# Decay exponents of a state-space layer: four products per tile instead of twelve, fed by small copies inside the on-chip memory

## The chip, the cores and the metric

The kernel runs on one core of a Trainium2 chip. The metric is the device time of one execution in microseconds, as the median over several runs. A profile was taken of one execution; its times count from the start of that execution's span. The engines are TensorE (PE, with its weight loads as PEld), VectorE (DVE), ScalarE (ACT), GpSimd (POOL) and SyncE (SP), which only issues transfers here. A "q" behind an engine's name is that engine's own queue of instructions that aren't computation.

## The reference

The input is 8 images of 32 x 32 positions with 128 channels, that is 8 sequences of 1024 tokens. Three layers follow each other.

1. A convolution layer with 1 x 1 kernels whose output attends to itself: q and v are two linear maps of the input, the scores are q times q transposed, and out = softmax(scores) v * gamma + input.
2. A state-space layer ("Mamba 2") over the normalised tokens, in residual form. Eight heads of 32 channels, a state of 32 per channel:

```python
def step(state, inp):
    dA_t, dt_t, B_t, C_t, x_t = inp
    state = state * dA_t[:, :, None, None] + (dt_t[:, :, None] * x_t)[..., None] * B_t[:, None, None, :]
    y = jnp.einsum('bhpn,bn->bhp', state, C_t)
    return (state, y)
```

with dA = exp(dt * -exp(A_log)), after a causal convolution over four tokens and a SiLU, and followed by a gated RMS norm and an output projection.

3. A mixture of 8 experts, the best two per token, with SiLU gating, again in residual form.

## The kernel before

The 8192 tokens are worked as 64 tiles of 128 tokens; 8 tiles (NT) make one sequence, called a batch here. Each engine runs its own program, with semaphores between them, and all of them walk through the same list of steps: step i of batch `base` does the scores of tile i, and, for tiles further back, the later stages. With i counted within the batch, `o = i - 1` is the tile of the attention output, `k = i - 6` the tile of the state-space products, `e = i - 7` the tile of its output, and in odd steps `d = i - 5` is the first of a pair of tiles whose decay sums are prepared. The order of the work within a step is written out by hand, engine by engine, and each engine runs strictly in that order.

The recurrence is worked in blocks of one tile. Within a tile, the contribution of key s to query t of head h carries the factor exp(cum[h, t] - cum[h, s]) for s <= t and 0 otherwise, where cum is the running sum of the decay exponents. The exponents for a whole tile are a matrix of 128 keys (partitions) by 8 heads x 128 queries, which TensorE makes in the PSUM bank pair pY; ScalarE exponentiates it into ED (L706); VectorE multiplies it with the tile's key-query products GT into M (L1365); TensorE uses the eight heads of M as weights against XDT (L433), adds the skip term (L437), and VectorE makes Y2 of it (L1266 or L1268), GpSimd YG.

The sums come in three bfloat16 parts that add up to the full value: C3 (VectorE, L1344 to L1358) is transposed by TensorE (L515), so that the three parts of 2 tiles x 8 heads lie on 48 partitions, and ScalarE copies it out twice, as CT3 (L715) and with the sign turned as NCT3 (L716), which raises the semaphore `ct3_ready`. This happens in an odd step; the two tiles of the pair use it in the next even and the next odd step.

Before the change the exponents are made by 12 matmuls per tile, at L454 to L460. Four matmuls of 256 columns have NCT3 as weights and the constant `pickm` as moving data: rows 0 to 47 pick the head's three parts, so that they add -cum[h, s] for every query, and rows 64 to 127 hold, for each half of the queries, a part of the mask: -1e30 where the key lies behind the query. Eight matmuls of 128 columns, one per head, have the constant `pick` as weights and CT3 as moving data, and add cum[h, t] for every key.

GpSimd builds all constants at the start (L829 to L883) and raises `consts` (identity and triangle), `masks` (awaited by ScalarE before its first step) and `iotas` (awaited by VectorE before its first step). SP's program (L249 to L368) loads the inputs, then, batch by batch, the next batch's xT once the present one's v product is done (`load_xT`) and the two halves of its X as the tiles of the attention output are finished (`x0_loaded`, `x1_loaded`); after the batches it fills the padding of the rows sorted by expert (`fill_up`, L307), fetches those rows for the experts (L322) and later the results for the final sum (L337). In the first part of the expert stage the last steps of the list are interleaved.

Other lines that are spoken of: the scores (L412 to L414) into pX, their maximum by VectorE (NM, L1243), the exponentials PR (ScalarE, L677), their transposes (L399) into pY, copied to PT (L648), the attention output (L483), the next batch's q product (L377) with its two parts QH (ScalarE, L637) and QL (VectorE, L1027), the transposes of YG (L467) copied to YT (ScalarE, L709), the output projection (L506), and the norm of two tiles, XN (ScalarE, L691).

Of the kernel before, what the change touches and what calls it, by code (L numbers as in the profile page):

```python
# [5 lines left out]
def conv_attn_ssm_moe(nc, x, xT, dw1, pw1, b1, dw2, pw2, b2, gamma, w_zdt, w_xbc, conv_w, conv_b,  # L6
# [3 lines left out]
    P = 128  # L10
    TILES = x.shape[0] // P
    NT = 8
# [26 lines left out]
    with ctx:  # L39
# [15 lines left out]
        HP = P // 2  # L55
        pickm = sb("pickm", [P, 16, HP], bf16)
        pick = sb("pick", [P, 16, P], bf16)
# [37 lines left out]
        CT3, NCT3 = sb("CT3", [P, 2, P], bf16), sb("NCT3", [P, 2, 2, P], bf16)  # L95
# [5 lines left out]
        ED, M = sb("ED", [P, H, P]), sb("M", [P, H, P])  # L101
# [61 lines left out]
        heads = lambda a: a[:].rearrange("p h t -> p (h t)")  # L163
        Y01 = [[PR[:], PT[:]], [heads(ED), heads(M)], [TR[:].rearrange("p t c -> p (t c)"), X[:].rearrange("p t c -> p (t c)")],
# [85 lines left out]
        def _(sp):  # L250
# [43 lines left out]
            for base in range(0, TILES - NT, NT):  # L294
                load_xT(base // NT + 1)
                sp.wait_ge(s("t_ready"), base + NT // 2)
                sp.dma_start(X[:, 0:NT // 2, :], xtok[:, base + NT:base + NT + NT // 2, :]).then_inc(s("x0_loaded"), 16)
                sp.wait_ge(s("t_ready"), base + NT)
                sp.dma_start(X[:, NT // 2:, :], xtok[:, base + NT + NT // 2:base + 2 * NT, :]).then_inc(s("x1_loaded"), 16)
# [71 lines left out]
        def _(pe):  # L371
# [13 lines left out]
            def step(base, i):  # L385
# [240 lines left out]
        def _(act):  # L626
# [12 lines left out]
            def step(base, i):  # L639
# [64 lines left out]
                if there(base, k):  # L704
                    upto(act, "d_ps", base, k + 1)
                    A(ED[:].rearrange("p h t -> p (h t)"), pY[:], ACT.Exp).then_inc(s("expD_ready"), 1)  # L706
# [123 lines left out]
        def _(pool):  # L830
# [8 lines left out]
            g.memset(pick[:], 0.0).then_inc(s("filled"), 1)  # L839
            pool.wait_ge(s("filled"), 2)  # L840

            g.affine_select(out=tri[:], in_=tri[:], compare_op=ALU.is_ge, fill=0.0, base=0, pattern=[[1, P]], channel_multiplier=-1)
            for j in range(3):
                g.affine_select(out=pick[:], in_=pick[:], compare_op=ALU.not_equal, fill=1.0, base=-16 * j,
                                pattern=[[-1, 16], [0, P]], channel_multiplier=1).then_inc(s("picked"), 1)
                pool.wait_ge(s("picked"), j + 1)
# [4 lines left out]
            g.memset(NCT3[:], 0.0)  # L851
            g.memset(pickm[:], 0.0).then_inc(s("masking"), 1)
            pool.wait_ge(s("masking"), 1)
            for th in range(2):
                last = g.affine_select(out=NCT3[:, :, th, :], in_=NCT3[:, :, th, :], compare_op=ALU.is_ge, fill=-1e30, base=HP * (th - 1),
                                       pattern=[[0, 2], [-1, P]], channel_multiplier=1)
            last.then_inc(s("masking"), 1)
            for j in range(3):
                g.affine_select(out=pickm[:], in_=pickm[:], compare_op=ALU.not_equal, fill=1.0, base=-16 * j,
                                pattern=[[-1, 16], [0, HP]], channel_multiplier=1).then_inc(s("masking"), 1)  # L860
                pool.wait_ge(s("masking"), j + 3)
            g.affine_select(out=pickm[:], in_=pickm[:], compare_op=ALU.not_equal, fill=1.0, base=-HP,
                            pattern=[[0, 16], [-1, HP]], channel_multiplier=1).then_inc(s("masking"), 1)
            pool.wait_ge(s("masking"), 6)
            g.memset(NCT3[0:HP], 0.0).then_inc(s("masks"), 1)
# [152 lines left out]
        def _(dve):  # L1018
# [198 lines left out]
            def step(base, i):  # L1217
# [143 lines left out]
                if there(base, k):  # L1361
# [3 lines left out]
                    tt(M[:], ED[:], GT[:, None, :].broadcast_to([P, H, P]), ALU.mult).then_inc(s("m_ready"), 1)  # L1365
# [208 lines left out]
```

## Time and profile before

| | |
|---|---|
| median of 3 runs | 1214.97 us (1214.96 to 1219.69) |
| span of the profiled execution | 1181.1 us, the only time that the page gives for it |
| TensorE matmul busy | 1083.7 us, 92% of the span |
| VectorE, ScalarE, GpSimd busy | 72%, 64%, 53% |
| first maximum of scores on VectorE | at 23.98 us |
| chain that ended last, by engine | PE 60%, DVE 11%, POOL 10%, issue 10%, ACT 3% |

The runs' time lies 33.9 us above the span: it holds what comes before the first and after the last instruction too. Busy time of TensorE is the time in which a matmul is in the pipeline, and successive matmuls overlap, so that the rows of the chain of waits (where each piece ends where the next begins) give what a matmul costs in sequence. "idle" in a row is the time in which the engine stood before that instruction, with the instruction that released it.

### The profile page before, as it was taken

The page shows a single profiled execution, that of the slowest core. Times are in us where ns is not written, and L with a number is a line of the kernel's source. Part 1 is how long each engine was busy: PE and PEld are TensorE (multiplying, and loading weights), DVE is VectorE, ACT ScalarE, POOL GpSimd, SP SyncE. Part 2 cuts the span into 40 slices and gives each one's busy share as a digit, 9 for nine tenths or more (in the row PEclk, how much of TensorE's full clock was granted, in tenths as well). Part 3 has the DMA queues.
Part 4 walks back from the last instruction along what each step waited for, and adds up shares of the span by engine and source line. Part 5 has one row for each costly group of instructions (what it writes and reads, how often), then busy time and mean ns, then how long its engine had stood idle before and what let it go on. Part 6 is the DMA issues. An engine that isn't in the chain of part 4 may idle for free.

```text
span 1181.1 us, 29643 instructions
## 1 busy us (share of the span) xinstructions
PE 1083.7 (92%) x8432; PEld 998.3 (85%) x8433; DVE 852.1 (72%) x3071; ACT 754.7 (64%) x1903; POOL 624.9 (53%) x981
## 2 busy tenths in 40 slices
PE   3889999999999999999999999867889999999993
PEld 2779888888988988988888888856789999999883
DVE  3488888988988888888898898776355644444564
ACT  1567777777767777767777777742476666666551
POOL 8122444467557566556646655743744665444442
PEclk9999999999999999999999999976799999999997
DMA  7200000001000100100100000010122222223666
GB/s 221 61 1 28 10 2 28 6 24 39 11 25 11 38 19 18 39 20 10 46 6 24 22 13 15 10 28 10 49 60 62 80 78 74 73 64 92 173 181 183
DMA packets 76439, 57.73 MB, mean 49 GB/s; under 512 B 10725, under 2 KB 70669, under 8 KB 76301
## 3 DMA queue, kind: packets, MB, share of 16 engines
q1 hardware_dynamic: 58285, 33.75, 10.5%
q0 software_dynamic: 8704, 17.97, 4.5%
q10 hardware_dynamic: 9312, 4.33, 1.3%
q8 instruction: 66, 1.08, 0.4%
q14 instruction: 72, 0.59, 0.2%
HBM read 32.27 MB, written 24.81 MB: 48 GB/s over the span
## 4 chain that ended last, share of the span: by engine, by line
PE 60%; DVE 11%; POOL 10%; issue 10%; ACT 3%; DMA 2%; SPq 2%; DVEq 1%; POOLq 0%; ACTq 0%
PE pc L433 7%; PE pY L588 7%; PE pX L583 6%; PE pa L483 5%; PE pb L600 3%; PE pd L600 3%; PE pY L399 3%; DVE CV L1232 2%; PE pc L437 2%; POOL rows_by_expert L991 2%; PE pX L412 2%; PE pa L444 2%; PE pX L414 2%; PE pX L413 2%; DMA GX<-rows_by_expert 2%
## 5 line engine op out<-in xcount | busy, mean ns | idle before, releaser
L1003 POOL DMA_INDIRECT results_by_choice<-YE,DIX x144 | 143.2, 995 | 147.6 <-ACT YE L786 132.5
L991 POOL DMA_INDIRECT rows_by_expert<-XA,SL x128 | 147.6, 1153 | 35.2 <-issue 35.2
L1481 DVE TENSOR_TENSOR V<-XT,pY 128x384 f32<-128x384 f32 x144 | 79.7, 554 | 116.1 <-ACT XT L777 111.5
L433 PEld LDWEIGHTS pc<-XDT,M 128*128 128x128 f32 x1024 | 128.3, 198 | 14.0 <-issue 9.5
L433 PE MATMUL pc<-XDT,M 128*128 128x64 f32 x1024 | 126.6, 279 | 6.4 <-DVE CT L1238 6.4
L1232 DVE SCALAR_TENSOR_TENSOR CV<-XBC,cw,CV 128x256 f32<-128x256 f32 x288 | 132.0, 513 | 0.0
L483 PE MATMUL pa<-V,PT 128*128 128x128 f32 x1024 | 127.3, 278 | 0.2 <-issue 0.2
L934 POOL TENSOR_TENSOR YG<-Y,SZ 128x256 f32<-128x256 f32 x64 | 46.5, 726 | 149.5 <-DVE Y L1266 135.7
L583 PE MATMUL pX<-TA,XBC 128*128 128x128 f32 (+1 forms) x864 | 121.2, 277 | 2.3 <-ACT TA L769 1.9
L588 PE MATMUL pY<-TA,XBC 128*128 128x128 f32 (+1 forms) x864 | 121.2, 277 | 1.2 <-DVE XBC L1485 1.0
L483 PEld LDWEIGHTS pa<-V,PT 128*128 128x128 f32 x1024 | 119.3, 192 | 2.7 <-issue 0.7
L1243 DVE TENSOR_REDUCE NM<-pX 128x1 f32<-128x1024 f32 x64 | 78.0, 1219 | 53.4 <-PE pX L414 52.1
L769 ACT ACTIVATE TA<-pa 128x128 f32<-128x128 f32 x144 | 39.8, 276 | 114.3 <-PE pa L576 113.5
L583 PEld LDWEIGHTS pX<-TA,XBC 128*128 128x128 f32 (+1 forms) x864 | 103.5, 181 | 3.0 <-ACT TA L769 2.5
L588 PEld LDWEIGHTS pY<-TA,XBC 128*128 128x128 f32 (+1 forms) x864 | 103.8, 182 | 2.6 <-DVE XBC L1485 2.5
L677 ACT ACTIVATE PR<-pX,NM 128x1024 f32<-128x1024 f32 x64 | 71.3, 1113 | 46.2 <-DVE NM L1243 46.1
L648 ACT ACTIVATE PT<-pY 128x1024 f32<-128x1024 f32 x64 | 65.4, 1022 | 40.2 <-PE pY L399 40.1
L1365 DVE TENSOR_TENSOR M<-ED,GT 128x1024 f32<-128x1024 f32 x64 | 78.6, 1228 | 12.8 <-ACT ED L706 12.1
L773 ACT ACTIVATE XBC<-W 128x341 f32 x144 | 71.3, 495 | 9.9 <-issue 9.8
L777 ACT ACTIVATE XT<-pX 128x384 f32<-128x384 f32 x144 | 69.9, 485 | 1.1 <-PE pX L583 1.1
L399 PE MATMUL pY<-ident,PR 128*128 128x128 f32 x512 | 67.9, 276 | 1.5 <-ACT PR L677 1.5
L925 POOL TENSOR_TENSOR STE<-ST,ETOT 32x256 f32<-32x256 f32 x56 | 40.0, 714 | 55.0 <-DVE ST L1432 54.9
(283 smaller groups left out, 2891.6 us busy)
## 6 DMA issues: line engine op xcount, KB each, us to landing
GX<-rows_by_expert SPq DMA_DIRECT2D x144, 65.0 KB, 1.8
XT<-in_xT_dram SPq DMA_DIRECT2D x8, 512.0 KB, 4.0
X<-in_x_dram SPq DMA_DIRECT2D x16, 256.0 KB, 3.0
out_dram<-T ACTq DMA_DIRECT2D x16, 256.0 KB
results_by_choice<-YE,DIX POOLq DMA_INDIRECT x144
rows_by_expert<-XA,SL POOLq DMA_INDIRECT x128, 2.4
XA<-results_by_choice SPq DMA_DIRECT2D x8, 256.0 KB, 5.1
W<-in_w1T_dram SPq DMA_DIRECT2D x1, 1364.0 KB
```

Of the source, the lines that this page charges most:

```text
L399: last = nc.tensor.transpose(pY[:, P * j:P * j + P], PR[:, P * j:P * j + P], ident[:])
L433: mm(pc[:, 64 * h:64 * h + 64], M[:, h, :], XDT[:, e % 2, HD * h:HD * h + 64], start=h == 0, stop=False, skip_group_check=True)
L483: last = mm(pa[:, 0:C], PT[:, P * j:P * j + P], V[:, j, :], start=j == 0, stop=j == NT - 1)
L583: last = mm(pX[0:hn, 512 * par + P * k:512 * par + P * k + P], WS[:, par, 0, h0:h0 + hn], GXT[:, par, :], start=True, stop=True, skip_grou ...
L588: last = mm(pY[0:hn, 512 * par + P * k:512 * par + P * k + P], WS[:, par, 1, h0:h0 + hn], GXT[:, par, :], start=True, stop=True, skip_grou ...
L677: A(PR[:], pX[:], ACT.Exp, bias=NM[:, i:i + 1], accum_out=RS[:, i:i + 1]).then_inc(s("exp_ready"), 1)
L991: g.indirect_dma_start(xg, bass.IndirectOffsetOnAxis(ap=SL[:, j // NT, j % NT:j % NT + 1], axis=0), XA[:, j // NT, j % NT, :], None).then_ ...
L1003: g.indirect_dma_start(yg, bass.IndirectOffsetOnAxis(ap=DIX[:, j, :], axis=0), YE[:, j, :], None).then_inc(s(f"ye{j}_scattered"), 16)
L1232: return stt(CV[:, m, :], XBC[:, m, fo + tap:fo + tap + 256], cw[:, m, tap:tap + 1], CV[:, m, :], ALU.mult, ALU.add)
L1243: v.tensor_reduce(NM[:, i:i + 1], pX[:], AX.X, ALU.max, negate=True).then_inc(s("nm_ready"), 1)
L1365: tt(M[:], ED[:], GT[:, None, :].broadcast_to([P, H, P]), ALU.mult).then_inc(s("m_ready"), 1)
L1481: tt(HT[:, par].rearrange("p k t -> p (k t)"), SH[:, par, :], pY[:, 512 * par:512 * par + HP3], ALU.mult).then_inc(s("hh_ready"), 1)
```

## The change

The exponents of a tile come from four matmuls, one per quarter of 32 queries, each with 8 heads x 32 queries = 256 columns. All three terms share the 128 contraction rows. Rows 0 to 47: NCT3 as weights against a pick of the head, as before. Rows 48 to 95: the weights are 1 and the moving tile RX holds the query sums themselves, each head's three parts in the columns of that head only and zeros elsewhere (a block layout). Rows 96 to 127: the mask for that quarter, a part in NCT3 and a part in RX. RX has 16 slots of 128 columns, for the two tiles of a pair and 8 heads each.

The query sums get into RX by DMA: for each pair of tiles SP waits for `ct3_ready` and issues 16 copies (`spread`), each of 3 rows of 256 bytes from CT3 to RX, and TensorE waits for all 16 (`cum_rows`) before the products. ED gets the order quarter, head, query; VectorE writes M in the old order, so M is written in runs of 32. NCT3 has four copies of the negated sums instead of two. `pick` and `pickm` and their preparation on GpSimd go; RX and four selects on it come, before the identity is built. SP's loads of the next batch stand among the copies in its queue.

```diff
-        pickm = sb("pickm", [P, 16, HP], bf16)
-        pick = sb("pick", [P, 16, P], bf16)
+        QT = P // 4
+        RX = sb("RX", [P, 16, P], bf16)
...
-        CT3, NCT3 = sb("CT3", [P, 2, P], bf16), sb("NCT3", [P, 2, 2, P], bf16)
+        CT3, NCT3 = sb("CT3", [P, 2, P], bf16), sb("NCT3", [P, 2, 4, P], bf16)
...
-        ED, M = sb("ED", [P, H, P]), sb("M", [P, H, P])
+        ED, M = sb("ED", [P, 4, H, QT]), sb("M", [P, H, P])
...
+            def spread(base, i):
+                if there(base, i - 5):
+                    if base + i == 5:
+                        sp.wait_ge(s("masks"), 1)
+                    sp.wait_ge(s("ct3_ready"), base + i - 3)
+                    for h2 in range(2 * H):
+                        sp.dma_start(RX[48 + h2:96:2 * H, h2, :], CT3[h2:48:2 * H, (i - 5) // 2 % 2, :]).then_inc(s("cum_rows"), 16)
+            for base in range(0, TILES + NT, NT):
+                loads = base < TILES - NT
+                if loads:
+                    load_xT(base // NT + 1)
+                spread(base, 1)
+                spread(base, 3)
+                if loads:
+                    load_x(base, 0)
+                spread(base, 5)
+                spread(base, 7)
+                if loads:
+                    load_x(base, 1)
...
-                    for h2 in range(2):
-                        four = pY[:, 512 * h2:512 * h2 + 512].rearrange("p (h t) -> p h t", h=4)
-                        for th in range(2):
-                            mm(four[:, :, HP * th:HP * th + HP], NCT3[:, par, th, :], pickm[:, half * H + 4 * h2:half * H + 4 * h2 + 4, :], start=th == 0, stop=False, skip_group_check=True)
-                    for h in range(H):
-                        last = mm(pY[:, P * h:P * h + P], pick[:, half * H + h, :], CT3[:, par, :], start=False, stop=True, skip_group_check=True)
+                    pe.wait_ge(s("cum_rows"), 16 * 2 * H * ((base + k) // 2 + 1))
+                    for q_ in range(4):
+                        last = mm(pY[:, H * QT * q_:H * QT * q_ + H * QT], NCT3[:, par, q_, :], RX[:, half * H:half * H + H, QT * q_:QT * q_ + QT], start=True, stop=True, skip_group_check=True)
...
-                    A(NCT3[0:48, dpar], pd[:, :].bitcast(bf16)[0:48, None, 0:P].broadcast_to([48, 2, P]), ACT.Copy, scale=-1.0).then_inc(s("ct3_ready"), 2)
+                    A(NCT3[0:48, dpar], pd[:, :].bitcast(bf16)[0:48, None, 0:P].broadcast_to([48, 4, P]), ACT.Copy, scale=-1.0).then_inc(s("ct3_ready"), 2)
...
-            g.memset(pick[:], 0.0).then_inc(s("filled"), 1)
+            g.memset(RX[:], 1.0).then_inc(s("filled"), 1)
...
+            g.affine_select(out=RX[:].rearrange("p a (q t) -> p (a q) t", t=QT), in_=RX[:].rearrange("p a (q t) -> p (a q) t", t=QT), compare_op=ALU.is_ge, fill=0.0, base=QT - P,
+                            pattern=[[0, 16 * 4], [-1, QT]], channel_multiplier=1).then_inc(s("picked"), 1)
...
-            g.memset(pickm[:], 0.0).then_inc(s("masking"), 1)
...
-            g.memset(NCT3[0:HP], 0.0).then_inc(s("masks"), 1)
+            g.memset(NCT3[0:P - QT], 1.0).then_inc(s("masks"), 1)
...
-                    tt(M[:], ED[:], GT[:, None, :].broadcast_to([P, H, P]), ALU.mult).then_inc(s("m_ready"), 1)
+                    tt(M[:].rearrange("p h (q t) -> p q h t", t=QT), ED[:], GT[:].rearrange("p (q t) -> p q t", t=QT)[:, :, None, :].broadcast_to([P, 4, H, QT]), ALU.mult).then_inc(s("m_ready"), 1)
```

## Rows read from the trace of the kernel before

**Rows 1.** The page, part 1: busy us, share of the span and instructions.

```profile
PE 1083.7 (92%) x8432; PEld 998.3 (85%) x8433; DVE 852.1 (72%) x3071; ACT 754.7 (64%) x1903; POOL 624.9 (53%) x981
```

**Rows 2.** Chain of waits, step 5 of a batch: start us, us, what.

```profile
437.77 0.44 PE pY L457 x4
438.21 0.45 PE pY L459 x8
```

**Rows 3.** Chain of waits, steps 3 and 0.

```profile
415.71 0.92 ACT ED L706
...
474.96 0.74 POOL YG L934
```

**Rows 4.** Timeline of ScalarE, step 5: start, duration, line, out<-in.

```profile
439.52 1.01 ACT L706 ACTIVATE ED<-pY 128x1024 f32<-128x1024 f32 x1
```

**Rows 5.** Timeline: VectorE in step 3, TensorE in step 7.

```profile
410.90 1.23 DVE L1243 TENSOR_REDUCE NM<-pX 128x1 f32<-128x1024 f32 x1 [0.20 <-PE pX L414]
...
456.67 0.47 PE L412 MATMUL pX<-QH 128*128 128x512 f32 x1 [0.44 <-DVE QL L1027]
```

**Rows 6.** Groups by line and form: shapes, count, busy us, mean ns.

```profile
L1365 DVE TENSOR_TENSOR M<-ED,GT 128x1024 f32<-128x1024 f32 x64 | 78.6, 1228 | 12.8 <-ACT ED L706 12.1 <-issue 0.6
...
L1266 DVE TENSOR_TENSOR Y<-pc,YO 128x256 f32<-128x256 f32 x56 | 23.3, 415 | 11.8 <-PE pc L437 11.4 <-DVE TBI L1214 0.2
...
L716 ACT ACTIVATE NCT<-pd 48x256 bf16<-48x256 bf16 x32 | 11.6, 363 | 0.0
```

**Rows 7.** Timeline of SP's queue: when an issue starts and how long it takes.

```profile
9.98 0.43 SPq L252 DMA_DIRECT2D hrow<-in_d_skip_dram  x1
10.46 0.91 SPq L252 DMA_DIRECT2D gw<-in_gnorm_w_dram  x2
...
431.66 0.37 SPq L297 DMA_DIRECT2D X<-in_x_dram  x1
...
784.69 10.05 SPq L307 DMA_DIRECT2D rows_by_expert<-padding_rows  x8
...
1126.15 0.60 SPq L337 DMA_DIRECT2D PT<-results_by_choice  x1
```

**Rows 8.** DMA landings: GX (line L322, us), then rT (KB, median us).

```profile
DMA to landing us min/median/max: 1.7/1.8/3.7
...
rT<-in_routerT_dram SPq DMA_DIRECT2D x1, 4.0 KB, 2.1
```

**Rows 9.** Timeline: negated copy in odd steps, first product of the next even step.

```profile
395.30 0.36 ACT L716 ACTIVATE NCT<-pd 48x256 bf16<-48x256 bf16 x1
...
403.32 0.60 PE L457 MATMUL pY<-pickm,NCT 128*128 128x256 bf16 x4
...
418.06 0.36 ACT L716 ACTIVATE NCT<-pd 48x256 bf16<-48x256 bf16 x1
...
426.76 0.60 PE L457 MATMUL pY<-pickm,NCT 128*128 128x256 bf16 x4
...
465.26 0.36 ACT L716 ACTIVATE NCT<-pd 48x256 bf16<-48x256 bf16 x1
...
474.52 0.60 PE L457 MATMUL pY<-pickm,NCT 128*128 128x256 bf16 x4
```

**Rows 10.** Timeline of the start: GpSimd's constants and VectorE's first maximum.

```profile
4.77 6.30 POOL L844 TENSOR_SCALAR_AFFINE_SELECT pick<-pick 128x2048 bf16<-128x2048 bf16 x3
...
12.56 0.95 POOL L852 MEMSET pickm<- 128x1024 bf16 x1
13.65 0.77 POOL L855 TENSOR_SCALAR_AFFINE_SELECT NCT<-NCT 128x256 bf16<-128x256 bf16 x2
14.38 3.73 POOL L859 TENSOR_SCALAR_AFFINE_SELECT pickm<-pickm 128x1024 bf16<-128x1024 bf16 x3
...
23.70 0.19 POOL L883 COPY OFF<-ebase 128x8 f32<-128x8 f32 x1
...
23.98 1.23 DVE L1243 TENSOR_REDUCE NM<-pX 128x1 f32<-128x1024 f32 x1 [1.16 <-issue]
```

More of the change, by code:

```diff
@@ L54, in conv_attn_ssm_moe @@
         trib, onesb = sb("trib", [P, P], bf16), sb("onesb", [P, P], bf16)
-        HP = P // 2
-        pickm = sb("pickm", [P, 16, HP], bf16)
-        pick = sb("pick", [P, 16, P], bf16)
+        QT = P // 4
+        RX = sb("RX", [P, 16, P], bf16)
         mhalf = sb("mhalf", [P, 2])
@@ L162, in conv_attn_ssm_moe @@
         rows_ = XA[:].rearrange("p a t c -> p (a t c)")
-        heads = lambda a: a[:].rearrange("p h t -> p (h t)")
-        Y01 = [[PR[:], PT[:]], [heads(ED), heads(M)], [TR[:].rearrange("p t c -> p (t c)"), X[:].rearrange("p t c -> p (t c)")],
+        Y01 = [[PR[:], PT[:]], [ED[:].rearrange("p q h t -> p (q h t)"), M[:].rearrange("p h t -> p (h t)")], [TR[:].rearrange("p t c -> p (t c)"), X[:].rearrange("p t c -> p (t c)")],
                [rows_[:, 0:SEQ], rows_[:, SEQ:2 * SEQ]]]
@@ L293, in load_xT, with load_x @@
                 sp.dma_start(XT[:], xT[n * P:n * P + P, :]).then_inc(s("xT_loaded"), 16)
[L294 to L299, printed above, removed]
+            def load_x(base, h):
+                sp.wait_ge(s("t_ready"), base + (h + 1) * NT // 2)
+                tiles = slice(h * NT // 2, (h + 1) * NT // 2)
+                sp.dma_start(X[:, tiles, :], xtok[:, base + NT + tiles.start:base + NT + tiles.stop, :]).then_inc(s(f"x{h}_loaded"), 16)
+            def spread(base, i):
[17 more added lines that the diff above has]
+                    load_x(base, 1)
             def fill_up(p_, experts):
@@ L705, in step @@
                     upto(act, "d_ps", base, k + 1)
-                    A(ED[:].rearrange("p h t -> p (h t)"), pY[:], ACT.Exp).then_inc(s("expD_ready"), 1)
+                    A(ED[:].rearrange("p q h t -> p (q h t)"), pY[:], ACT.Exp).then_inc(s("expD_ready"), 1)
                 if there(base, e):
@@ L838, in _ @@
             g.memset(tri[:], 1.0)
-            g.memset(pick[:], 0.0).then_inc(s("filled"), 1)
+            g.memset(RX[:], 1.0).then_inc(s("filled"), 1)
             pool.wait_ge(s("filled"), 2)
             g.affine_select(out=tri[:], in_=tri[:], compare_op=ALU.is_ge, fill=0.0, base=0, pattern=[[1, P]], channel_multiplier=-1)
+            g.affine_select(out=RX[:].rearrange("p a (q t) -> p (a q) t", t=QT), in_=RX[:].rearrange("p a (q t) -> p (a q) t", t=QT), compare_op=ALU.is_ge, fill=0.0, base=QT - P,
+                            pattern=[[0, 16 * 4], [-1, QT]], channel_multiplier=1).then_inc(s("picked"), 1)
+            pool.wait_ge(s("picked"), 1)
             for j in range(3):
-                g.affine_select(out=pick[:], in_=pick[:], compare_op=ALU.not_equal, fill=1.0, base=-16 * j,
+                g.affine_select(out=RX[:], in_=RX[:], compare_op=ALU.not_equal, fill=1.0, base=-16 * j,
                                 pattern=[[-1, 16], [0, P]], channel_multiplier=1).then_inc(s("picked"), 1)
-                pool.wait_ge(s("picked"), j + 1)
+                pool.wait_ge(s("picked"), j + 2)
             g.affine_select(out=ident[:], in_=ident[:], compare_op=ALU.not_equal, fill=1.0, base=0, pattern=[[-1, P]], channel_multiplier=1).then_inc(s("filled"), 1)
@@ L850, in _ @@
             g.tensor_copy(identb[:], ident[:]).then_inc(s("consts"), 1)
-            g.memset(NCT3[:], 0.0)
-            g.memset(pickm[:], 0.0).then_inc(s("masking"), 1)
+            g.memset(NCT3[:], 0.0).then_inc(s("masking"), 1)
             pool.wait_ge(s("masking"), 1)
-            for th in range(2):
-                last = g.affine_select(out=NCT3[:, :, th, :], in_=NCT3[:, :, th, :], compare_op=ALU.is_ge, fill=-1e30, base=HP * (th - 1),
+            for q_ in range(4):
+                last = g.affine_select(out=NCT3[:, :, q_, :], in_=NCT3[:, :, q_, :], compare_op=ALU.is_ge, fill=-1e30, base=QT * q_ + QT - P,
                                        pattern=[[0, 2], [-1, P]], channel_multiplier=1)
             last.then_inc(s("masking"), 1)
[L858 to L864, printed above, removed]
-            g.memset(NCT3[0:HP], 0.0).then_inc(s("masks"), 1)
+            pool.wait_ge(s("masking"), 2)
+            g.memset(NCT3[0:P - QT], 1.0).then_inc(s("masks"), 1)
             g.memset(EXPERT[:], 0.0).then_inc(s("iotas"), 1)
```

## The prediction

> **What bounds the kernel now.** I read the page's busy line first [rows 1]: TensorE is busy 92% of the span, which says where to look but not what a saved matmul is worth. The change touches every step of the eight attention batches, so I then read the chain of waits over one batch. It alternates. From 423 to 450 us (steps 4, 5, 6) and from 476 us on (steps 0, 1, 2 of the next) it is TensorE alone, instruction after instruction, and the decay product stands in it with 0.44 us (L457) and 0.45 us (L459) [rows 2]. In step 3, and from step 6 to the next step 0, it leaves TensorE for ScalarE, VectorE and GpSimd [rows 3]: there a shorter product gives back nothing by itself. So the saving must not be multiplied by 64 tiles.
>
> Two more limits come from the engine timelines. In odd steps ScalarE runs through XN, SQ, ED and YT in that order without a gap: in step 5 ED starts at 439.52, although the product was over at 438.66 [rows 2, 4]. TensorE's L506 waits for YT, so an odd step's product can end 0.45 us sooner and move nothing on that path. In step 2 VectorE is full with routing: the max over the next scores starts only 0.20 us after VectorE was free [rows 5], so a quicker TensorE alone gains at most about 0.2 us there.
>
> **The change, part by part.** *Products.* Per tile, 4 matmuls of 256 columns and 8 of 128 go (0.89 us of chain), and 4 of 256 columns remain, 0.44 us by L457's own row [rows 2]. That saves 0.45 us a tile: 28.8 us over 64 tiles if TensorE set the time everywhere (one end), nothing where the chain is elsewhere (the other). I count it in full in steps 2 and 4, where it is set off against the new wait below, and 0.1 us a batch for the odd steps.
>
> *VectorE and ScalarE.* M is now written in runs of 32 elements. VectorE has such runs already: Y2 (L1266), 256 elements in runs of 32, takes 415 ns, and M 1228 ns for 1024 [rows 6], 1.06 ns for each further element, so I take 0 for the runs; if each cost something, it would stand under the 0.20 us of step 2 first. The negated copy grows from 256 to 512 columns: 363 ns for 256 (L716), about 1010 for 1024 (ED) [rows 4, 6], hence +0.21 us, once a pair. It delays the signal that the new DMAs wait for; what ScalarE does behind it then waits for TensorE anyway.
>
> *The new DMAs.* For each pair of tiles SP issues 16 copies, and TensorE waits for all of them before the even tile's product. Nothing of the kind is in the trace, so I build the chain: signal to issue, 15 spacings, landing of the last.
> - Signal: 0.09 us, as from GpSimd's OFF copy (ends 23.89) to VectorE's first max (23.98) [rows 10].
> - Spacing: a lone load takes 0.37 us to issue; with 0.04 us between two, 0.41 is the low end. Small loads back to back at the start stand 0.48 us apart, and the two behind them take 0.91 together. A 256 KB load late in the kernel takes 0.60 [rows 7]; I take 0.55 as the high end. The tiny ones back to back are nearest in kind: 0.475.
> - Landing: GX (65 KB) takes 1.7 us at best and 1.8 in the median, the small rT 2.1 [rows 8]; I take 1.8, between the two ends.
>
> From the end of the old negated copy to the data: 0.21 + 0.09 + 15 x 0.475 + 1.8 = 9.2 us (ends: 8.1 and 10.6).
>
> A rule speaks against such copies: the Trainium skill, "DMA: Bandwidth & Descriptors", Rules for kernel authors, says to coalesce many small transfers, since below 64 KB one pays mostly overhead; its section on the anatomy of one DMA puts the fixed part at about 2.0 us, fitted on the GpSimd path. With 2.0 for the landing the chain would be 9.4 us and the sum below about 4 us larger; GX's 1.8 decides here.
>
> What time is there? From the end of L716 to L457 of the next even step [rows 9]: 403.32 − 395.66 = 7.66 us from step 1 to 2, 8.34 from 3 to 4, 8.90 from 7 to 0; from 5 to 6 it is as from 1 to 2, and the seven full batches repeat this within 0.3 us. So, per batch:
> - step 2: 9.2 − 7.66 = 1.54 us of standing TensorE, less 0.45 of shorter product: +1.1;
> - step 4: 9.2 − 8.34 = 0.86, less 0.45: +0.4;
> - step 6: +1.1 again, but TensorE already waits 0.44 us for QL before the next scores [rows 5], and QL comes from VectorE, whose M waits for the softplus and not for ED; I count 0.65 hidden: +0.4;
> - step 0: 9.2 − 8.90 = 0.3, hidden: the product ends at 474.52 + 0.89 = 475.41, and L467 behind it waits for YG until 475.70 [rows 3, 9];
> - odd steps: −0.1.
>
> That is +1.8 us a batch, +12.6 for seven. The first batch has only its last two pairs, and a lightly loaded VectorE: +1. Behind TensorE's wait stand L467, the attention output (L483) and all that follows in order, then ED, YT and M.
>
> *SP's queue.* The loads of X and xT and the fill of the padding now stand behind copies. The X load of this batch is issued at 431.66 [rows 7]; step 3's copies are out by 418.42 + 0.3 + 16 x 0.475 = 426.3, so it isn't moved. The padding fill (8 issues in 10.05 us from 784.69 [rows 7]) now starts behind the copies of step 67, some 30 us later; the first fetch of rows waits for it, perhaps 0 to 2 us longer (a landing), while TensorE is still in the last steps: taken 0.
>
> *Start.* GpSimd's constants set it: the first max follows the OFF copy at once [rows 10]. Out go the memset of pickm (0.95) and its four selects (3.73 x 4/3 = 4.97); in comes one select of 2048 columns (6.30 / 3 = 2.1), and NCT3's share doubles in columns: +0.77 for two more selects, about +0.5 for each of two memsets (half of 0.95) [rows 10]. Net 5.92 − 3.87 = −2.05 us; 0 if something else were late next.
>
> *Tail.* Steps 64 to 70 hold the last six products: at most 6 x 0.45 = −2.7, and three waits as above; I take −1.5.
>
> Sum: 12.6 + 1 − 2.05 − 1.5 = +10 us on the span of 1181.1. The page gives the profiled execution no time but its span; the median of the runs lies 33.9 us above it, which I carry over unchanged: 1215 + 10 = **1225 us**.
>
> **The rivals.**
> 1. *The copies are hidden.* It decides below a chain of about 8.2 us (spacing 0.41, landing 1.8). For: 0.37 us is all that a lone issue takes, and three rows of 256 B are less than any load here. Against: no run of issues in the trace is that tight. Per batch −0.45 (step 4), −0.2 (step 2), −0.1: −5 for seven, start and tail −3.5: 1206.5. The Trainium skill, same page, section "Issuing engines are not separate DMA queues", says that issue time is usually small against the DMA itself; by that the copies would be there after a few us, which is this rival. The trace speaks against it here: 16 issues of 0.48 us against one landing of 1.8.
> 2. *TensorE sets the time everywhere:* −28.8 − 2: about 1184. Against it, rows 3 to 5.
> 3. *The copies come just in time:* spacing 0.42 to 0.46, chain 8.4 to 8.95, per batch −0.2 to +1.0: 1211 to 1220.
> 4. *Issue is dearer:* spacing 0.55, landing 2.1: chain 10.6, steps 2, 4, 6 and 0 cost about 2.5, 1.8, 1.8 and 0.9: +48 for seven batches, +3 for the first, −3.5: about 1262.
>
> **How the numbers follow.** Each 0.01 us of spacing moves the sum by about 3.2 us (0.15 us in three steps of seven batches), so the spacing is the forecast. About 0.5% (6 us) is what a measurement of this kernel can tell from no change. Chances: forecast (chain 9.0 to 10.0) 0.39, rival 4 0.07, rival 3 0.30, rival 1 0.20, rival 2 0.04. Faster is rivals 1 and 2, 0.24; within 0.5% rival 3, 0.30; slower 0.46. The range runs from rival 1's 1207 to the 1248 of a spacing of 0.53; the forecast's own is 1221 to 1245.
>
> **What would show it.** In the profile after: four matmuls of 256 columns a tile, about 0.44 us; 512 copies issued by SP, 0.475 us apart; in TensorE's waits a DMA into RX before the even products, about 1.5, 0.9, 1.5 and 0.3 us in steps 2, 4, 6 and 0; a first max near 21.9 us; M still near 1.23 us. A spacing under 0.42 us, or a landing near 1 us, makes me wrong towards faster; a spacing over 0.53 towards slower. A TensorE clock that fell during the new waits would be outside all of this.

## The result, and the profile after

The changed kernel takes 1370.28 us (median of 4 runs, 1368.91 to 1371.77) against 1215.36 us for the kernel before: ratio 1.127, 95% interval 1.125 to 1.129. It is 155 us slower; the prediction had said 1225 us, 1207 to 1248.

The profiled execution has a span of 1367.4 us, 2.9 us under the median. In the profile of before this distance was 33.9 us; that one execution was some 30 us shorter than the timed ones, all of it behind the attention batches (351.8 us from the start of the last M to the end, against 376.7 to 386.6 us in the profiles of the kernel after and of all those below). So the 33.9 us are not what comes before the first and after the last instruction, as was said ahead of the prediction; in the profiled run of the kernel after, time and span differ by 1.75 us (1369.15 and 1367.4). The two traces are therefore compared over the attention stage, by the start of the last of the 64 M (the last number in M's rows): 829.3 us before, 982.6 us after, +153.3 us, all but some 2 us of the loss.

The page of the kernel after, part 1 and the granted clock of part 2 (in tenths, 40 slices of the span); the first line answers to [rows 1]:

```profile
PE 1120.4 (82%) x7920; PEld 1024.2 (75%) x7921; DVE 855.3 (63%) x3071; ACT 759.0 (56%) x1903; POOL 612.1 (45%) x979
...
PEclk9998999998999989999889999996589999999997
```

TensorE has 512 matmuls fewer and is busy 37 us longer. The waits of TensorE (what it waited for, us in total, times, longest):

```profile
PE pY L475 <- DMA RX<-CT: 127.4, 32, 5.6
```

All 32 pairs wait for the copies. The chain of waits over one pair (start us, us, what), from the end of the negated copy to the product; the twelve issues left out are like those shown:

```profile
438.99 0.58 ACT NCT L732
439.58 0.02 issue
439.59 0.64 SPq L305
440.23 0.04 issue
440.28 0.64 SPq L305
...
449.15 0.64 SPq L305
449.79 0.04 issue
449.83 1.63 DMA RX<-CT
451.46 0.14 issue
451.60 0.59 PE pY L475 x2
```

Each issue holds SP for 0.64 us and the next one starts 0.04 us later. The sixteenth starts at 449.83, where the row of its transfer begins: 15 spacings in 10.24 us, 0.683 us each. Its data is in use 1.63 + 0.14 = 1.77 us later. From the end of the negated copy (439.57) to the product it is 12.0 us, where [rows 9] left 7.7 to 8.9 us from the end of the shorter one. This is a pair whose even tile comes in step 0; its wait is 3.19 us. Now TensorE behind this wait, in the timeline:

```profile
448.02 0.39 PE L464 MATMUL pa<-CTP,SX 128*128 128x128 f32 x2
451.60 1.01 PE L475 MATMUL pY<-RX,NCT 128*128 128x256 bf16 x4 [3.19 <-DMA RX<-CT]
452.40 0.63 PE L483 MATMUL pb<-ident,YG 128*128 128x128 f32 x2
452.83 2.83 PE L499 MATMUL pa<-V,PT 128*128 128x128 f32 x16
...
464.06 0.60 PE L475 MATMUL pY<-RX,NCT 128*128 128x256 bf16 x4
...
465.36 1.96 PE L499 MATMUL pa<-V,PT 128*128 128x128 f32 x16
```

In the even tile the same four products take 1.01 us and the attention output (L499) 2.83 us; in the odd tile, which finds its data there, 0.60 and 1.96 us. The windows say why (busy time of each engine, then the granted clock, DMA share and GB/s):

```profile
448.40:451.60 3.20, 0.01 (x2) 0.04 (x2) 2.88 (x24) 1.17 (x5) 2.50 (x5) 0.95 0.01 1
451.60:454.80 3.20, 3.20 (x16) 3.02 (x17) 1.62 (x4) 2.16 (x5) 1.62 (x2) 0.52 0.17 47
454.80:464.00 9.20, 9.20 (x75) 8.83 (x74) 4.92 (x16) 6.55 (x12) 2.69 (x8) 1.00 0.27 87
```

After 3.19 us without a matmul the granted clock was 0.52 for the next 3.2 us, that is the lower level, 1.2 GHz, almost throughout; then it was back at 1.00 (2.4 GHz). So two suspects stand: the wait itself, and the clock behind it.

The timelines that answer to [rows 9] and [rows 10] (the longer negated copy; the first maximum of the scores), and then M by its line, in the kernel before and after, which answers to [rows 6]:

```profile
438.99 0.58 ACT L732 ACTIVATE NCT<-pd 48x512 bf16<-48x512 bf16 x1
...
22.23 1.23 DVE L1255 TENSOR_REDUCE NM<-pX 128x1 f32<-128x1024 f32 x1 [0.46 <-DVE diagD L1482]
```

```profile
L1365 DVE TENSOR_TENSOR M<-ED,GT x64: 1205/1226/1287, 73.9 to 829.3; 128x1024 f32<-128x1024 f32 x64
...
L1377 DVE TENSOR_TENSOR M<-ED,GT x64: 1205/1226/1289, 77.7 to 982.6; 128x1024 f32<-128x1024 f32 x64
```

The negated copy has grown as said, and M has not (the median is the second of the three durations, in ns; behind them stand the first and last start).

### The profile page after: what moved, and what is told of

It reads as the page before. It is cut to its first block, busy times and chain, and to the rows that moved or that the text cites. A ratio compares the mean times of both kernels' runs of the same rounds, so it can differ in the third digit from the quotient of the medians.

```text
span 1367.4 us, 29158 instructions
## 1 busy us (share of the span) xinstructions
PE 1120.4 (82%) x7920; PEld 1024.2 (75%) x7921; DVE 855.3 (63%) x3071; ACT 759.0 (56%) x1903; POOL 612.1 (45%) x979
## 4 chain that ended last, share of the span: by engine, by line
PE 37%; SPq 23%; issue 14%; POOL 9%; DMA 6%; ACT 4%; DVE 4%; another core or an unknown queue 3%; POOLq 0%; ACTq 0%; DVEq 0%
SPq L305 22%; PE pa L499 10%; PE pX L599 5%; PE pY L604 5%; DMA RX<-CT 4%; PE pb L522 3%; PE pb L616 2%; PE pY L475 2%; POOL st L986 2%; PE pd L616 2%; PE pb L483 2%; POOL YG L946 2%; ACT NCT L732 1%; PE pa L592 1%
## 5 line engine op out<-in xcount | busy, mean ns | idle before, releaser
L499 PE MATMUL pa<-V,PT 128*128 128x128 f32 x1024 | 159.8, 322 | 0.0
L1003 POOL DMA_INDIRECT rows_by_expert<-XA,SL x128 | 142.6, 1114 | 35.2 <-issue 35.2
L499 PEld LDWEIGHTS pa<-V,PT 128*128 128x128 f32 x1024 | 156.6, 241 | 0.5 <-issue 0.2
L475 PE MATMUL pY<-RX,NCT 128*128 128x256 bf16 x256 | 52.1, 342 | 127.4 <-DMA RX<-CT 127.4
L599 PE MATMUL pX<-TA,XBC 128*128 128x128 f32 (+1 forms) x864 | 124.6, 281 | 21.6 <-ACT TA L785 19.8
L722 ACT ACTIVATE ED<-pY 128x1024 f32<-128x1024 f32 x64 | 65.1, 1017 | 121.1 <-PE pY L475 121.1
L475 PEld LDWEIGHTS pY<-RX,NCT 128*128 128x128 bf16 x256 | 26.7, 113 | 138.1 <-issue 132.7
L983 POOL TENSOR_SCALAR st<-MV 128x2 f32<-128x2 f32 x32 | 6.2, 192 | 206.5 <-DVE MV L1425 206.5
```

Source lines behind the costliest of these rows:

```text
L475: last = mm(pY[:, H * QT * q_:H * QT * q_ + H * QT], NCT3[:, par, q_, :], RX[:, half * H:half * H + H, QT * q_:QT * q_ + QT], start=True, ...
L499: last = mm(pa[:, 0:C], PT[:, P * j:P * j + P], V[:, j, :], start=j == 0, stop=j == NT - 1)
L599: last = mm(pX[0:hn, 512 * par + P * k:512 * par + P * k + P], WS[:, par, 0, h0:h0 + hn], GXT[:, par, :], start=True, stop=True, skip_grou ...
L1003: g.indirect_dma_start(xg, bass.IndirectOffsetOnAxis(ap=SL[:, j // NT, j % NT:j % NT + 1], axis=0), XA[:, j // NT, j % NT, :], None).then_ ...
```

## The experiments

Theory 1: the issue time of 512 small copies on SP makes the chain 12 us long, TensorE waits for it once a pair, and the lower clock behind each wait adds the rest. The rivals: that the copies or the new product are dear in themselves, whoever waits; that the clock has no part; and, for the size of an issue, several causes.

**Waiting for fewer copies.** First the copies stay and only what a tile waits for changes.

```diff
-  sp.dma_start(RX[48 + h2:96:2 * H, h2, :], CT3[...]).then_inc(s("cum_rows"), 16)
+  sp.dma_start(RX[48 + h2:96:2 * H, h2, :], CT3[...]).then_inc(s(f"cum_rows{h2 // H}"), 16)
-  pe.wait_ge(s("cum_rows"), 16 * 2 * H * ((base + k) // 2 + 1))
+  pe.wait_ge(s(f"cum_rows{half}"), 16 * H * ((base + k) // 2 + 1))
```

> The edit: the 16 copies of a pair signal two semaphores, 8 copies each, and a tile's decay product waits only for the 8 that bring its own heads. Nothing else changes. Theory 1 (the time is lost in the wait of the even tile's product for 16 issues of SP, 0.683 us apart, and in the lower TensorE clock behind that wait): the chain from the end of the negated copy becomes 0.02 + 7 x 0.683 + 1.77 = 6.6 us, below the 7.45 us that step 2 leaves (7.66 less 0.21 for the longer negated copy), so the wait on the copies goes to nearly 0 in all 32 pairs, the odd tile has a whole step more for the other 8, the granted clock goes back to about 0.97, and the time comes near the 1206.5 us that the prediction gave for hidden copies (1203 to 1212). Rival 2 (512 small copies, or the new product and the strided write of M, are themselves dear, whoever waits): the wait goes, but the time stays over 1230 us, with the loss spread over rows that do not follow the wait. Rival 3 (it is the wait alone, the clock has no part): same time as theory 1, since with the wait the clock's loss goes too; the next kernels tell these apart.

Measured: 1211.76 us against 1211.95, ratio 0.9996 (0.9979 to 1.0014). The wait on the copies is gone from the list, SP still issues all 512 at 0.64 us each, and the last M starts at 828.6 us. So the copies, the new product and the strided M together cost nothing by themselves: the wait, with what hangs on it, is the whole loss. But the 1206.5 us of hidden copies did not come either; more on that below.

Then a chain of the length that the prediction had assumed:

```diff
-  .then_inc(s("cum_rows"), 16)
+  .then_inc(s("cum_rows" if h2 < 12 else "last_rows"), 16)
-  pe.wait_ge(s("cum_rows"), 16 * 2 * H * ((base + k) // 2 + 1))
+  pe.wait_ge(s("cum_rows"), 16 * 12 * ((base + k) // 2 + 1))
+  if half == 1:
+      pe.wait_ge(s("last_rows"), 16 * 4 * ((base + k) // 2 + 1))
```

> The edit: an even tile's product waits for the first 12 of the 16 copies (more than it needs, its own are the first 8), the odd tile's for the last 4 as well. The chain then is 0.02 + 11 x 0.683 + 1.77 = 9.3 us, which is the 9.2 us that the prediction had taken for all 16: this asks whether its turning of a chain into time was right, once the chain has the length that it assumed. By the prediction's sum (stalls of 1.5, 0.9, 1.5 and 0.3 us in steps 2, 4, 6 and 0, each less what the shorter product gives) the time is about 10 to 20 us over the kernel before, 1222 to 1232 us, with the granted clock at about 0.96. Theory 1a (each wait also lowers TensorE's clock for some us behind it): waits of 0.6 to 1.9 us may be too short to lower the clock, and then the two agree; if they lower it, the time is 1240 to 1280 us and the granted clock 0.92 to 0.94. If the time were nearly that of the kernel before, the available time would have been under-read.

Measured: 1246.69 us, ratio 1.0285 (1.0259 to 1.0311): +34 us, more than the prediction's sum gives for that chain. Windows of two batches of this kernel, each as long as from the M of a batch's tile 5 to that of the next, and 8.5 us behind it:

```profile
445.00:542.80 97.80, 89.83 (x650) 80.17 (x649) 82.85 (x299) 70.72 (x166) 57.55 (x99) 1.00 0.07 24
542.80:644.20 101.40, 92.57 (x645) 82.65 (x644) 83.30 (x299) 70.12 (x166) 57.13 (x99) 0.97 0.07 23
```

With the clock at 1.00 a batch is 97.8 us long, 2.4 more than the 95.4 us that lie between the same two M of the kernel before. Where the clock fell somewhere, it is 101.4. TensorE's waits around the first window, in steps 4, 6, 0 and 2:

```profile
447.73 0.60 PE L477 MATMUL pY<-RX,NCT 128*128 128x256 bf16 x4 [1.00 <-DMA RX<-CT]
472.06 0.60 PE L477 MATMUL pY<-RX,NCT 128*128 128x256 bf16 x4 [1.74 <-DMA RX<-CT]
496.25 0.60 PE L477 MATMUL pY<-RX,NCT 128*128 128x256 bf16 x4 [0.45 <-DMA RX<-CT]
521.77 0.60 PE L477 MATMUL pY<-RX,NCT 128*128 128x256 bf16 x4 [1.75 <-DMA RX<-CT]
```

The prediction had said 0.9, 1.5, 0.3 and 1.5 us, for a chain 0.3 us shorter as it counts. The prediction's steps give +2.7 us a batch for this chain of 9.3 us, counted from the end of the longer copy, so that 7.66 − 0.21 = 7.45 us are there in step 2 (step 2: 9.3 − 7.45 − 0.45 = 1.4; step 4: 0.7; step 6: 1.4 − 0.65 = 0.75; step 0 hidden; −0.1). Its way from a chain to a time was right where the clock stayed at 1.00; over the whole kernel its steps give some +17 us (2.75 for each of seven batches, +1 and −3.5 for the rest), and the other half of the +34 us goes with the clock: the two batches at 1.00 are 2.4 us longer than in the kernel before, the others, each at a lower clock than there, 4.0 to 7.2 us.

**The clock alone.** TensorE gets something to do while it waits, so that the wait stays and the fall of the clock goes.

```diff
+  if half == 0:
+      for j in range(14):
+          nc.tensor.transpose(pY[:, P * (j % NT):P * (j % NT) + P], ident[:], ident[:])
   pe.wait_ge(s("cum_rows"), 16 * 2 * H * ((base + k) // 2 + 1))
```

> The edit: ahead of the wait for the copies TensorE does 14 transposes of the identity into the buffer that the decay product then overwrites, in even tiles only, so that most of the wait is filled with matmul work; the copies and the wait's end stay where they are. Theory 1a (behind each wait TensorE runs some 3 to 7 us at the lower clock, and that is about a third of the loss): the granted clock of the attention stretch goes back toward 0.97 to 1.00, the attention output L499 (now about 322 ns in the mean) goes back to about 280 ns, and the time falls from 1370 to about 1310 to 1335 us although TensorE has more to do and the wait for the copies ends as late as before. Rival 3 (the wait alone makes the loss, the clock has no part): the time stays at 1370 us or rises by what the transposes overrun.

Measured: 1330.81 us, ratio 1.0971 (1.0938 to 1.1004), last M at 949.4 us. With 448 transposes more to do, TensorE is there 982.6 − 949.4 = 33 us sooner. More than half of the wait is left (70.7 of the 127.4 us, up to 3.3 at a time), so:

```diff
-      for j in range(14):
+      for j in range({0: 37, 2: 26, 4: 37, 6: 31}[k % NT]):
```

> The edit: as with the 14 transposes, but with 37, 26, 37 and 31 of them ahead of the waits of the four pairs of a batch, 0.121 us each, so that the transposes end about when the copies land. Theory 1a: with 14 the clock was back to 0.97 to 0.98 in the attention stretch and the loss at about 119 us; with the wait filled it is at 1.00, and the time is that of the wait alone, 1315 to 1331 us, with almost no wait on the copies left in the list of waits. The prediction's formula with the measured chain of 12.0 us gives about +13 us a batch, some +100 in all, 1312 us. Rival: the transposes put off the product themselves, and the time rises over 1335 us.

Measured: 1314.42 us, ratio 1.0835 (1.0804 to 1.0867), last M at 928.7 us; 12.9 us of the wait are left. M's row, and a batch of this kernel in the windows:

```profile
L1380 DVE TENSOR_TENSOR M<-ED,GT x64: 1203/1225/1292, 77.4 to 928.7; 128x1024 f32<-128x1024 f32 x64
...
408.00:516.20 108.20, 103.97 (x781) 94.32 (x780) 83.14 (x298) 70.93 (x166) 56.67 (x100) 1.00 0.07 21
```

The clock is at 1.00 in all of it, and a batch takes 108.2 us, +12.8. So of the 153 us of the attention stage, 928.7 − 829.3 = 99 us are the wait, and the other 982.6 − 928.7 = 54 us went when TensorE was kept busy in it: the clock. The rival without the clock is out.

**What makes an issue take 0.64 us.** Four kernels. In the first two the rows of a copy change: 48 neighbouring rows (in which every head's exponents hold the sums of all heads), and the three rows of a head placed side by side.

```diff
-  sp.dma_start(RX[48 + h2:96:2 * H, h2, :], CT3[h2:48:2 * H, two, :])
+  sp.dma_start(RX[48:96, h2, :], CT3[0:48, two, :])                          # 48 rows
+  sp.dma_start(RX[48 + 3 * h2:51 + 3 * h2, h2, :], CT3[3 * h2:3 * h2 + 3, two, :])  # neighbours
```

> The edit: each of the 16 copies moves 48 neighbouring rows (all heads) to its column of the right-hand tile in place of 3 rows with a stride of 16. It changes what is computed: each head's decay exponent then holds the sums of all heads. The count of copies, the waits and the instructions of the other engines stay. Question: what makes an issue take 0.64 us and the spacing 0.683 us. Theory A (copies of three rows are dear because so few rows give little to spread over the DMA engines, or because of the row stride): the issue falls to 0.37 to 0.45 us, the chain to about 8.3 us, the waits nearly vanish and the time comes under 1230 us. Theory B (it is the price of any such copy within SBUF, or of issues back to back, whatever the rows): issue and spacing stay at 0.64 and 0.68 us, the chain at 12 us and the time at 1370 us, or higher if 16 times the bytes land later.

> The edit: the contraction rows are put in another order, so that the three parts of one head's sum stand on neighbouring rows and each copy moves 3 neighbouring rows in place of 3 rows with a stride of 16. The same result, the same count of copies and bytes. Theory A' (the row stride makes the issue dear, as more than one block has to be described): the issue falls from 0.64 to about 0.4 to 0.5 us, the chain to 8.5 to 9.5 us, and the time to 1210 to 1250 us. Theory B (the stride has no part): 0.64 us, chain 12 us, 1370 us.

Measured: 1361.21 us (1.122) and 1367.87 us (1.128). The same line of the issues in the first, then in the second kernel (ns min/median/max):

```profile
L305 SPq DMA_DIRECT2D RX<-CT x512: 503/592/1812, 63.4 to 961.9; - x171
```

```profile
L305 SPq DMA_DIRECT2D RX<-CT x512: 639/640/823, 62.8 to 971.2; - x171
```

Sixteen times the rows made an issue 0.05 us cheaper; the kernel took 1359.65 and 1362.78 us in its two runs, against 1365.70 and 1370.04 us with neighbouring rows. The stride has no part. In the third the sums go to DRAM first and the 16 copies read them there:

```diff
+  sp.dma_start(ctd[two], CT3[0:48, two, :]).then_inc(s("sums_saved"), 16)
+  sp.wait_ge(s("sums_saved"), 16 * n)
   for h2 in range(2 * H):
-      sp.dma_start(RX[48 + h2:96:2 * H, h2, :], CT3[h2:48:2 * H, two, :]).then_inc(s("cum_rows"), 16)
+      sp.dma_start(RX[48 + h2:96:2 * H, h2, :], ctd[two, h2:48:2 * H, :]).then_inc(s("cum_rows"), 16)
```

> The edit: SP first saves the 48 rows of sums to DRAM with one copy, waits for it, and the 16 copies then read their 3 rows from DRAM instead of from SBUF. Theory C (the source within SBUF makes the issue dear; loads from DRAM took 0.35 to 0.37 us when alone): the 16 issues take 0.37 to 0.45 us each and the chain, with one more copy and landing in front of it (about 2.5 us), comes to about 11 us: time 1300 to 1350 us. Theory B (any small copy costs this on SP, one behind another): issue 0.64 us, spacing 0.683 us, chain 14.5 us, time 1430 to 1480 us.

Measured: 1423.62 us (1.174). The issues, from DRAM now:

```profile
L309 SPq DMA_DIRECT2D RX<-sums x512: 629/630/775, 64.1 to 1027.5; - x171
```

For copies of 3 rows the source has no part either (0.63 us against 0.64); other sizes were not compared. The time is a little under the 1430 us that theory B began at. The fourth adds nine copies of other sizes behind the 16 of each pair, on top of the kernel in which a tile waits for its own 8:

> The edit: the kernel in which a tile waits for its own 8 copies, plus nine copies on SP behind the 16 of each pair, of data that nothing reads: within SBUF 256 B rows to 1, 16, 32, 64 and 128 partitions, a second one of 128 partitions, 3 rows of 16 B, and to DRAM 128 rows and 3 rows of 256 B. What each issue takes is read from the trace. So far: 3 rows of 256 B 0.64 us from SBUF and 0.63 us from DRAM, 48 rows 0.59 us, 48 rows of 4 KB 0.70 us, but 128 rows of 2 or 4 KB 0.35 to 0.37 us, and 48 rows to DRAM 0.31 us. Theory P (a destination of fewer than 128 partitions of SBUF is the dear case): 1 to 64 partitions 0.55 to 0.70 us, 128 partitions about 0.37 us, both stores to DRAM about 0.31 us. Theory Q (the size in bytes, small ones dear): 1 row and 3 rows of 16 B the dearest, 128 rows of 256 B no cheaper than 48 rows. The time stays within 0.5% of the kernel before, since SP has 13 us free in each pair.

Measured: 1217.81 us, ratio 1.0027 (1.0009 to 1.0045). SP's queue in one pair of it; within SBUF 1 and 128 rows of 256 B (16, 32 and 64 rows, left out between them, took 0.58 to 0.59 us), to DRAM 128 and 3 rows, within SBUF 128 rows once more, and 3 rows of 16 B:

```profile
453.03 0.56 SPq L313 DMA_DIRECT2D G<-identb  x1
...
455.52 0.60 SPq L317 DMA_DIRECT2D G<-identb  x1
456.16 0.59 SPq L318 DMA_DIRECT2D far<-identb  x1
456.80 0.30 SPq L319 DMA_DIRECT2D far<-identb  x1
457.15 0.62 SPq L320 DMA_DIRECT2D G<-trib  x1
457.81 0.75 SPq L321 DMA_DIRECT2D G<-identb  x1
```

The theory of few destination partitions falls: 128 of them take 0.60 us. That small copies are the dear ones holds only at its end: 3 rows of 16 B are the dearest, but one row of 256 B isn't. Nor do rows and bytes alone set the time: over all 32 pairs the second copy of 128 rows (L320) took 0.487 us in the median, the first (L317) 0.597. What makes the 3 rows to DRAM take 0.30, and the 128-row load of X 0.37 [rows 7], stays open. For this kernel it is enough that none of the forms of copy into RX that were tried was under 0.5 us.

**Fewer issues.** One copy puts the sums on the diagonal blocks of a zeroed area in DRAM, a second brings the whole block layout (48 rows of 4 KB, 192 KB in the trace's count) back.

```diff
-  for h2 in range(2 * H):
-      sp.dma_start(RX[48 + h2:96:2 * H, h2, :], CT3[...]).then_inc(s("cum_rows"), 16)
+  sp.dma_start(bank_[two].rearrange("j (h x) -> j h x", h=2 * H)[:, :, 0:P], CT3[0:48, two, :]).then_inc(s("sums_saved"), 16)
+  sp.wait_ge(s("sums_saved"), 16 * (n + 2))
+  sp.dma_start(RX[48:96].rearrange("p a t -> p (a t)"), bank_[two, :, 0:2 * H * 2 * H * P].rearrange("j (h x) -> j h x", h=2 * H)).then_inc(s("cum_rows"), 16)
```

> The edit: per pair, two copies in place of 16. One writes the 48 rows of sums to the diagonal blocks of a zeroed area in DRAM, the other brings the whole block layout (48 rows of 4 KB, 196 KB) back into the right-hand tile. Theory 1 (the count of issues made the chain long): chain 0.02 + 2 x 0.64 + 2 landings of 1.8 to 2.9 = 5 to 7 us, under the 7.45 us at hand, no waits on the copies, granted clock as before, and the time equal to the kernel before within 0.5%, as with the wait for a tile's own 8 copies: since there every tile's M began within 0.1 us of the kernel before up to tile 55, a shorter decay product is worth nothing here. Rival (bytes matter: 256 times as many per pair into RX): landings over 4 us, waits of 1 to 3 us in steps 2 and 6, time over 1240 us.

Measured: 1214.52 us, ratio 1.0012 (0.9988 to 1.0037). The two issues of a pair, in SP's queue:

```profile
441.43 0.30 SPq L309 DMA_DIRECT2D block_rows<-CT  x1
443.37 0.71 SPq L311 DMA_DIRECT2D RX<-block_rows  x1
```

TensorE waits for the data 4 times in all, 2.3 us together: 16 times the bytes of a pair, fetched by way of DRAM, are there sooner than 16 small copies. (The 256 times in the text before the run are one large copy against one small one; the 16 small ones bring 12 KB together.) Copies shared out between SP and the queue of another engine were not tried.

**What a shorter product is worth.** With the waits gone the time is that of the kernel before. TensorE in an odd step, first of the kernel before, then of the one that waits for its own 8:

```profile
437.61 0.60 PE L457 MATMUL pY<-pickm,NCT 128*128 128x256 bf16 x4
438.04 0.61 PE L459 MATMUL pY<-CT,pick 128*128 128x128 bf16 x8
438.63 0.44 PE L467 MATMUL pb<-ident,YG 128*128 128x128 f32 x2
```

```profile
437.59 0.60 PE L475 MATMUL pY<-RX,NCT 128*128 128x256 bf16 x4
438.61 0.44 PE L483 MATMUL pb<-ident,YG 128*128 128x128 f32 x2 [0.42 <-POOL YG L946]
```

The transposes of YG start at the same moment. GpSimd's YG in the kernel before, and the wait for it in the one that waits for its own 8:

```profile
437.85 0.73 POOL L934 TENSOR_TENSOR YG<-Y,SZ 128x256 f32<-128x256 f32 x1 [1.91 <-DVE Y L1266]
```

```profile
PE pb L483 <- POOL YG L946: 25.1, 59, 1.6
```

YG ended at 437.85 + 0.73 = 438.58 us in the kernel before, just as the old product did: a tie, which shows no idle time. The 0.45 us went into waiting for YG, 25.1 us in 59 waits against 5.5 us in 10 before. Theory 4 was that other work in this gap would turn them into time; the state product (0.43 us) can stand there.

```diff
   last.then_inc(s("d_ps"), 1)
+  if not decays and k % NT != 0:       # even tiles; in the second kernel without "not decays"
+      upto(pe, "st_ready", base, k)
+      upto(pe, "yo_ready", base, k)
+      if front_b:
+          upto(pe, "u_ready", base, fb + 2)
+      mm(pd[:, 0:DI], CTP[:, par, tk], ST[:], start=True, stop=True)
```

> The edit: a tile waits for its own 8 copies, and in even tiles the state product (current C times the state, 0.43 us) moves from behind the attention output to right behind the decay product, where TensorE stood 0.3 to 0.4 us for GpSimd's YG. Theory 4 (the 0.45 us that the shorter decay product frees went into the wait for YG, since YG comes in the same moment in which the old product ended): the wait L483 <- YG goes from 25 us to about 13, TensorE is 0.43 us ahead behind the attention output of even tiles, and the time falls by 3 to 13 us against the kernel before. Rival (another engine sets the step anyway; ScalarE and VectorE run through from ED to M): no change, within 0.3%.

> The edit: as in the even tiles, in odd ones too; there the transposed sums get another place in their PSUM buffer, so that the state product can stand before them. Theory 4: the wait for YG goes to about nothing, and the time falls by 6 to 25 us against the kernel before. Rival: no change, since in odd steps ScalarE runs from XN through SQ and ED to YT without a gap.

> The edit: the kernel before, with the old decay product of 0.89 us, and the same move of the state product in even and odd tiles. It says what the move gives without the shorter product. Theory 4: in the kernel before there is no gap to fill (TensorE waits 5.5 us for YG in all), so the move only puts the transposes of YG off by 0.43 us, and the time is the same within 0.3% or up to 1% longer. Rival: the move itself is what gains, and the time falls as much as with the shorter product.

Measured: even tiles 1212.0 us, 0.9970 (0.9952 to 0.9989); both 1210.23 us, 0.9965 (0.9952 to 0.9978); the old product with the move 1209.89 us, 0.9959 (0.9945 to 0.9972), against 1214.79. From the first M to the last it takes 755.4 us in the kernel before, 754.8 with own 8 copies, 752.1 with the move in even tiles, 749.4 with the move in all tiles, and 749.7 with the move and the old product. So the move gains some 0.4%, the shorter product nothing on top of it: the gain in even tiles lies at the lower edge of theory 4's range, but the theory is wrong, and the rival of the third kernel is right. TensorE of the kernel with the move in all tiles, in an even step:

```profile
429.94 0.47 PE L431 MATMUL pX<-QH 128*128 128x512 f32 x1 [0.36 <-DVE QL L1043]
```

Here 0.36 us of what was freed turn up in front of the scores, in a wait for VectorE's QL. Over the whole run this wait is 7.3 us in 14 times, against 5.5 us in 9 in the kernel before, so it holds only a small part of what was freed; where the rest went stays open. The old product with the state product moved is thus as fast as any version found; why the move helps there stays open too.

## Why the prediction was wrong

**The step that failed** is the spacing in the part on the new DMAs: "The tiny ones back to back are nearest in kind: 0.475", with 0.55 as the high end. It measured 0.683. A late load had taken 0.60 and the padding fills stood 1.26 us apart (10.05 / 8) [rows 7]; 0.60 + 0.04 as the high end would have given a chain of 11.7 us. The true chain is 12.0 us from the end of the longer copy, 12.2 as the prediction counts, in place of 9.2. With it the prediction's own steps, each a wait less what it gives back, come to 12.03 − 7.45 − 0.45 = 4.1 us (step 2), 3.45 (step 4), 4.1 − 0.65 = 3.5 (step 6), 2.6 (step 0: the product ends at 474.52 + 3.34 + 0.44 = 478.30, 2.6 us behind the 475.70 of YG) and −0.1, together 13.6 us a batch; the kernel with the wait filled measured 12.8. The waits in these sums, 4.6, 3.9, 4.6 and 3.3 us, measured 4.5, 3.8, 4.2 and 3.5 us in the kernel after (batch from 538 us on). The 3.2 us by which each 0.01 us of spacing was to move the sum left step 0 out, which is no longer hidden at this length.

**What it left outside** was the clock, named in its last sentence as such and given no price: 54 of the 153 us. The right spacing alone would therefore not have saved the sum: with nearly the chain that it had assumed the kernel came out at +34 us, where the prediction's steps give some +17. The Trainium skill, "TensorE: Matmul & The Clock Gate", section Why this matters for your kernels, advises against idle gaps of TensorE between bursts of matmuls for this reason; the 0.52 behind the wait of 3.19 us agrees.

**What was right.** Landing 1.8 us (1.63 + 0.14 = 1.77); the signal, 0.02 us where 0.09 was taken; the negated copy +0.21 us (0.58 against 0.36); M unchanged (median 1226 ns in both traces); the first maximum at 22.23 us (21.9 said); the wait in front of the even products and none in front of the odd ones.

**What was too high** is the gain where nothing waits for the copies. Set off against a wait, the 0.45 us held: the four waits shown above give 1.30 (step 2), 0.55 (step 4) and 0.64 (step 6), step 0 hidden, and with the −0.1 that is 2.39 us, the 2.4 us of that batch. Without a wait the product ends before YG is there. The prediction saw YG only in step 0; the tie in the other steps takes away the gains of rivals 1 and 2. So of the rival of hidden copies, 1206.5 us, the mechanism came true with a tile's own 8 copies, but not its gains: 1211.8 against 1212.0.

**The rules weighed.** Coalescing small transfers, as the Trainium skill, "DMA: Bandwidth & Descriptors", Rules for kernel authors, advises, was the right rule: two copies leave 2.3 us of wait where 16 small ones leave 127.4. That issue time is usually small against the DMA itself, as the section "Issuing engines are not separate DMA queues" of the same page of the Trainium skill says, does not hold here: 16 issues of 0.64 us stand against one landing of 1.77.

## What to carry to other kernels

Many small copies that one instruction waits for are a serial chain on the issuing queue: multiply their number by the dearest small issue that the trace shows, and either let each consumer wait for its own share or bring the data in few large copies. A wait of several us on TensorE costs more than its length, because what stands behind it may run at half the clock; look at the granted clock of the windows behind a wait before calling the wait the whole loss. And an engine that runs without idle time is not yet the bound: look whether another engine's result arrives in the same moment, because then a shorter instruction only makes a wait.

## What the runs showed of the hardware that was not expected

- An issue of the copies tried on SP took from 0.30 us (3 rows of 256 B to DRAM) to 0.75 us (3 rows of 16 B within SBUF) in the median. The number of rows had hardly any effect (1 to 128 rows of 256 B within SBUF: 0.555 to 0.597 us, but 0.487 us for the second copy of 128 rows), and for 3 rows neither the row stride nor the source had one; which property decides was not found.
- Behind a wait of TensorE of 3.19 us the granted clock was 0.52 for 3.2 us (shown above). In the kernel that waits for 12 copies it was 0.57 from 324 to 328 us, behind a wait of 2.90 us, and 1.00 from 472 to 476 us, behind one of 1.74 us. But it was 0.57 from 621 to 625 us as well, behind another wait of 1.74 us, so that the length of a wait alone does not tell whether the clock falls. With transposes in the waits it was 1.00 in the batch shown.
